# Reordered SBUF reservations in a macaron block: where TensorE's operands start

## The reference

```
x = x + 0.5 * ffn(layernorm(x))
x = x + attention(layernorm(x))
x = x + 0.5 * ffn(layernorm(x))

ffn(x):  h = silu(x @ W1 * s1) * (x @ W2 * s2)      # 256 -> 1024
         h = gelu(h @ H1 * t1)                      # 1024 -> 1024
         h = gelu(h @ H2 * t2)                      # 1024 -> 1024
         return h @ W3 * s3                         # 1024 -> 256
```

## The kernel before

| array | role in TensorE | before | after |
|---|---|---|---|
| `w_in`, `wring` | stationary, float32r | 128 | 128 |
| `fT_hi`, `fT_lo` | moving, float32r | 480 | 128 |
| `h_hi`, `h_lo` | moving in the hidden layers, stationary in the output layer | 480 | 128 |
| `w_out3` | moving in the output layer | 128 | 704 |
| `wproj`, `wo` | moving, float32 | 128 | 128 |
| `aT`, `zT`, `z`, `a_hat` | float32: stationary, transposed, or moving in the first pass | 800 | 128 |
| `f_hat` | transposed | 480 | 128 |
| `xf` | none (DMA, VectorE, ScalarE) | 480 | 128 |
| `slot0` to `slot3` | first pass's weights only; else DMA, VectorE, GpSimd | 800 | 128 |

## Time and profile before

### The profile page before, as it was taken

One profiled execution on the slowest core, in us unless ns is written; L12 is line 12 of the kernel. 1 busy time (PEld: TensorE's weight loads), 2 busy tenths in 40 slices (PEclk: granted clock), 3 DMA queues, 4 the chain that ended last, 5 costly groups with the idle time before them and its releaser, 6 DMA issues.

```text
span 1608.1 us, 19160 instructions
## 1 busy us (share of the span) xinstructions
PE 1528.4 (95%) x6978; PEld 1224.9 (76%) x6978; DVE 1086.0 (68%) x1475; ACT 677.6 (42%) x1062; POOL 553.3 (34%) x402
## 2 busy tenths in 40 slices
PE   7689999999999999999999999999999999998998
PEld 6567888777777778787777877768788877786887
DVE  6323758894777686777876877778675978793322
ACT  7434445344343435344534353434343444352442
POOL 2003051535171607162526070533614245434020
PEclk9899999999999999999999999999999999999999
DMA  7662848666766494857765757557474776754332
GB/s 308 252 241 101 281 140 302 224 207 226 232 234 218 155 312 142 279 171 262 261 229 183 251 182 261 185 192 254 157 265 158 269 247 223 269 198 157 118 100 71
DMA packets 189218, 342.41 MB, mean 213 GB/s; under 512 B 15552, under 2 KB 138560, under 8 KB 188736
## 3 DMA queue, kind: packets, MB, share of 16 engines
q1 hardware_dynamic: 189120, 341.13, 62.1%
HBM read 319.05 MB, written 30.41 MB: 217 GB/s over the span
## 4 chain that ended last, share of the span: by engine, by line
PE 66%; DVE 12%; POOL 8%; DMA 7%; ACT 4%; issue 3%; SPq 0%; DVEq 0%; POOLq 0%; ACTq 0%
PE f_bank L1101 22%; PE f_bank L1102 22%; PE a_banks L1179 6%; PE f_bank L1030 4%; PE f_bank L1031 4%; DMA weights_hi<-in_ffn_w 3%; POOL acc L693 3%; PE f_bank L1130 2%; PE f_bank L1131 2%; DVE slot L935 2%; DVE slot L979 2%; DVE S L941 2%; POOL acc L690 2%; PE a_banks L1199 1%; POOL h_lo L707 1%
## 5 line engine op out<-in xcount | busy, mean ns | idle before, releaser
L1101 PE MATMUL f_bank<-h_hi,wring 128*128 128x512 f32 x2048 | 824.4, 403 | 31.1 <-POOL h_lo L707 12.4
L1102 PE MATMUL f_bank<-h_lo,wring 128*128 128x512 f32 x2048 | 813.6, 397 | 0.0
L1101 PEld LDWEIGHTS f_bank<-h_hi,wring 128*128 128x128 f32 x2048 | 387.6, 189 | 131.9 <-issue 18.4
L1102 PEld LDWEIGHTS f_bank<-h_lo,wring 128*128 128x128 f32 x2048 | 387.6, 189 | 93.2 <-issue 1.4
L773 ACT ACTIVATE h_hi<-f_bank,colv 128x512 fp32r<-128x512 f32 x256 | 176.5, 689 | 553.1 <-PE f_bank L1102 552.9
L895 DVE TENSOR_TENSOR h_lo<-f_bank,h_hi 128x512 fp32r<-128x512 f32 x256 | 175.2, 687 | 258.5 <-ACT f_bank L774 256.8
L707 POOL TENSOR_TENSOR h_lo<-f_gated,h_hi 128x512 fp32r<-128x512 f32 x128 | 165.4, 1305 | 449.1 <-ACT h_hi L767 448.3
L1030 PE MATMUL f_bank<-fT_hi,w_in 128*128 128x512 f32 x480 | 197.5, 411 | 11.6 <-ACT f_gated L762 5.4
L1031 PE MATMUL f_bank<-fT_lo,w_in 128*128 128x512 f32 x480 | 191.5, 399 | 0.0
L979 DVE TENSOR_TENSOR slot<-slot,a_banks 128x1280 f32<-128x1280 f32 (+4 forms) x124 | 169.5, 1375 | 21.1 <-DMA slot<-keys_and_values 20.7
L935 DVE TENSOR_TENSOR slot<-slot,a_banks 128x1280 f32<-128x1280 f32 (+4 forms) x124 | 170.5, 1375 | 17.0 <-DMA slot<-keys_and_values 16.8
(11 more groups left out here) (117 smaller groups left out, 1328.1 us busy)
## 6 DMA issues: line engine op xcount, KB each, us to landing
wring<-weights_hi SPq DMA_DIRECT2D x256, 512.0 KB, 4.6
slot<-keys_and_values SPq DMA_DIRECT2D x128, 384.0 KB, 4.9
slot<-keys_and_values SPq DMA_DIRECT2D x64, 640.0 KB, 4.0
slot<-keys_and_values SPq DMA_DIRECT2D x312, 128.0 KB, 4.4
slot<-keys_and_values SPq DMA_DIRECT2D x64, 256.0 KB, 5.7
weights_hi<-in_ffn_w SPq DMA_DIRECT2D x16, 512.0 KB, 5.0
keys_and_values<-kv_out SPq DMA_DIRECT2D x32, 256.0 KB, 2.3
xf<-in_x SPq DMA_DIRECT2D x8, 512.0 KB, 5.8
```

Of the source, the lines that this page charges most:

```text
L1101: pe.matmul(bank[:, :], hi, h_hi[src][:, k, :], start=(k == 0), stop=False)
L1102: last = pe.matmul(bank[:, :], hi, h_lo[src][:, k, :], start=False, stop=(not general and k == KH - 1))
```

## The change

The order of the `sb(...)` calls is changed, and with it where each array starts; no array's size, and no instruction, is changed. The arrays whose sizes are whole KB are reserved first, and the small ones after them. `ident` (512 bytes), `half_neg` (16 bytes, taking 32) and `flag` (4 bytes, taking 32) come ahead of `w_out3`, which so starts 576 bytes further beyond a whole KB than the rest. The words that come with the change call the first arrays "at whole KB" and `w_out3` "64 bytes past one"; by adding up the sizes they are all 128 bytes past a whole KB, and `w_out3` is 704 past one.

```diff
--- before.py
+++ after.py
@@ -165,19 +165,11 @@
             return ctx.enter_context(nc.semaphore(name))
 
 
+
         w_in = sb("w_in", [P, IN_BLOCKS, WBLK], fp32r)
-        w_out3 = sb("w_out3", [P, OUT_BLOCKS, WBLK], fp32r)
         wring = sb("wring", [P, 4, WBLK], fp32r)
         wproj = sb("wproj", [P, KD, 4 * D])
         wo = sb("wo", [P, KD, D])
-        colv = sb("colv", [P, 4 * KH])
-        rowv = sb("rowv", [P, 6 * D + HEADS * (NU + NT)])
-        ident = sb("ident", [P, P])
-        differ = sb("differ", [P, BLOCKS])
-        differ_sum = sb("differ_sum", [P, 1])
-        ones = sb("ones", [P, 1])
-        flag = sb("flag", [1, 1], mybir.dt.int32)
-        half_neg = sb("half_neg", [P, NB])
 
         xf = sb("xf", [P, 2, NB, D])
         f_hat = sb("f_hat", [P, NB, D])
@@ -186,12 +178,6 @@
         h_hi = [sb(f"h_hi{i}", [P, KH, TT], fp32r) for i in range(2)]
         h_lo = [sb(f"h_lo{i}", [P, KH, TT], fp32r) for i in range(2)]
         f_gated = sb("f_gated", [P, 3, TT])
-        f_st = sb("f_st", [P, NB, 6])
-        f_mo = sb("f_mo", [P, 5, NB])
-        f_mean = sb("f_mean", [P, NB])
-        f_shift = sb("f_shift", [P, NB])
-        f_var = sb("f_var", [P, NB])
-        f_rs = sb("f_rs", [P, NB])
 
         xa = sb("xa", [P, 2, SB, D])
         aT = sb("aT", [P, KD, ST])
@@ -199,12 +185,19 @@
         kv_out = sb("kv_out", [P, SB, 2, D])
         slots = [sb(f"slot{g}", [P, GS, D]) for g in range(4)]
         a_hat = sb("a_hat", [P, SB, D])
-        S = sb("S", [P, SB, HEADS, NU])
         acc = sb("acc", [P, GS, D])
         z = sb("z", [P, SB, D])
         zT = sb("zT", [P, KD, ST])
 
         first_T = [aT, zT]
+        ident = sb("ident", [P, P])
+
+        half_neg = sb("half_neg", [P, NB])
+        flag = sb("flag", [1, 1], mybir.dt.int32)
+        w_out3 = sb("w_out3", [P, OUT_BLOCKS, WBLK], fp32r)
+        colv = sb("colv", [P, 4 * KH])
+        rowv = sb("rowv", [P, 6 * D + HEADS * (NU + NT)])
+        S = sb("S", [P, SB, HEADS, NU])
         merge = sb("merge", [P, 3, HEADS, NT])
         a_st = sb("a_st", [P, SB, 6])
         a_mo = sb("a_mo", [P, 5, SB])
@@ -214,6 +207,15 @@
         a_rs = sb("a_rs", [P, SB])
         mx = sb("mx", [P, SB, HEADS])
         sm = sb("sm", [P, SB, HEADS])
+        f_st = sb("f_st", [P, NB, 6])
+        f_mo = sb("f_mo", [P, 5, NB])
+        f_mean = sb("f_mean", [P, NB])
+        f_shift = sb("f_shift", [P, NB])
+        f_var = sb("f_var", [P, NB])
+        f_rs = sb("f_rs", [P, NB])
+        differ = sb("differ", [P, BLOCKS])
+        differ_sum = sb("differ_sum", [P, 1])
+        ones = sb("ones", [P, 1])
 
         fb = [ctx.enter_context(nc.psum_tensor(f"f_bank{i}", [P, 512], fp32)) for i in range(4)]
         pairs = [ctx.enter_context(nc.psum_tensor(f"a_banks{i}", [P, WBLK], fp32)) for i in range(2)]
```

## The result

The changed kernel takes 1588.38 us, the median of four runs (1587.78 to 1590.15); the kernel before took 1611.9 us in the runs beside it (1610.43 to 1613.33). The ratio is 0.9861, with a 95% interval of 0.9847 to 0.9875: 23.5 us or 1.4% less. The profiled execution took 1588.57 us.

What follows compares the result with a forecast made beforehand. PE's pace was taken to bound the kernel, a third of the span hanging on attention and transfers. 1609.98 - 28.4 gave 1581.6 us, 1582 us on the runs' scale, all else counted at nothing; range 1541 to 1613 us.

Steps and rivals of the forecast that it cites:

- What bounds the kernel: Whole kernel: PE, busy 95% of 1608.1 us, sets the end; a third of the span hangs on attention and transfers.
- Step 1: Hidden and input layers: moving operands going from 480 to 128 save 8.0 ns a matmul, bounds nothing to 17.3 ns.
- Theory A: Experiments' expectation: the moving operand's start within a 64-byte piece costs one more piece of 16 columns, 6.7 ns.
- Step 2: Chain: 3549 hidden and input matmuls at 8.0 ns shorten the path by 28.4 us; the other 1507 count nothing.
- Step 3: Output layer: w_out3 from 128 to 704, h from 480 to 128; counted at nothing, bound 6.4 us either way.
- Step 4: Everything else that moves (xf, xa, gate, kv_out, slots, acc): counted at nothing, a few us of gain as bound.
- Nothing happens: Rival, all float32r matmuls: columns are fed slightly slower than one per cycle wherever they start; 1611 us, chance 0.28.
- The whole excess goes: Rival, hidden, input and output layers: distance between moving and stationary starts matters, up to 17.3 ns a matmul; 1541 us, chance 0.17.
- Slower: Rival, hidden and input layers: streams starting at the same offset meet and wait, 8.0 ns a matmul; 1639 us, chance 0.13.

Runs made afterwards that it cites:

- both_crooked: The changed kernel with fT, h, w_in and wring, both operands of the hidden and input layers, at 160 instead of 128: 1588.06 us.
- weights_crooked: The changed kernel with the weights w_in and wring alone 32 bytes further, at 160 instead of 128: 1610.19 us.
- weights_64: The changed kernel with the weights w_in and wring alone 64 bytes further, at 192, fT and h at 128: 1610.56 us.
- moving_64: The changed kernel with the moving arrays fT and h alone 64 bytes further, at 192, weights at 128: 1599.83 us.
- moving_only: The kernel before with only xf, f_hat, fT, h and f_gated moved from 480 to 128; w_out3 and the attention's arrays stay: 1592.42 us.
- moving_crooked: The changed kernel with the moving arrays fT and h alone 32 bytes further, at 160 instead of 128: 1609.65 us.

## Why the prediction was right, and where not

**What bounds the kernel** held. PE's pace was what the change touched, no other engine's sum moved, and the difference in PE's busy time, 29.6 us, is more than the difference in the span, 21.4.

**Step 1, the price and its reason.** The size was near: forecast 8.0 ns a matmul, measured 6.7 in steady rows (233.3 to 226.7). Over the run it is less still: the hidden average went from 233.4 to 227.1 ns, 6.2, the input layer's from 233.4 to 228.6, 4.8, because a row of matmuls does not start at its new pace. In the trace of the kernel after, the first step behind float32 work or behind a break (a step of 260 ns or more) averages 232 to 235 ns, the fourth 228 to 230, and from about the tenth on it is 227. 4096 x 6.2 + 960 x 4.8 ns = 30.0 us, which is PE's 29.6. The reason was wrong. "I take them for the start" is the sentence that failed: the 8.0 ns between the output layer's excess and the hidden layer's are no price of a crooked moving operand. both_crooked has both operands crooked and runs at 226.7 ns; weights_crooked has a straight moving operand and runs at 233.3. What counts is the distance between the two starts. Theory A's 6.7 ns hit the number, but no run shows its reason, and two refute its condition: both_crooked has the moving operand 32 bytes past a multiple of 64 and runs at 226.7 ns, weights_64 has every start on a multiple of 64 and runs at 233.3. Why the difference is 6.7 ns, no run shows. The kernel after profits because its distance is 0; with its weights 32 bytes off (weights_crooked) the steps are 233.3 ns and the time is 1610.19 us.

**Step 2, what of it shortens the path.** It said that 3549 of 5056 matmuls, 0.70, would shorten the span. Measured: 21.4 of 29.6 us in the two profiles, 0.72; by the medians 23.5 of 30.0, 0.78. With the prices averaged over the run, 2998 x 6.2 + 551 x 4.8 ns = 21.2 us; the interval of the measured gain is 20.1 to 24.7 us. One pair of profiles is little to go by, but PE's idle time (span less busy) tells the same in all 14 kernels: 86.0 to 88.9 us, 87.0 on average, in the six with a hidden distance of 0, and 79.7 to 83.4 us, 81.3 on average, in the seven with hidden averages of 232.7 ns or more (moving_64 has 86.3). By that 5.7 of the 29.6 us are lost in waits, and the share is 0.8. So the step was right in kind and a little low. What was to be late next, the attention's chain and the ring's fills, is in the waits: GpSimd, `a_hat`, the ring's transfers. One of its signs did not come: the chain shares of VectorE and GpSimd were to rise, and they are 11% for 12% and 8% as before; it is the hidden layers' share that rose, from 43.5 to 44.3%. The 2998 hidden matmuls counted on the old chain are therefore not a fixed set.

**Step 3, the output layer at nothing:** 118.7 to 117.9 ns at the end, 118.2 to 117.8 on average, 0.2 us over the 596 matmuls of its chain share. But for its own reason: with `w_out3` left at 128 it would have gone to 119.9 (moving_only). The distance of 576, 64 within 256, saves those 2 ns, 1.2 us on the same 596 matmuls.

**Step 4, everything else at nothing:** held as far as it shows. With the hidden and input layers' distance at 32 and all other arrays at their new place the time is the old one (moving_crooked, 1609.65 us). The transfers into the slots, which start at 128 instead of 800 now, land their 384 KB in 4.7 us instead of 4.9, and not a good 1 us sooner; those into the ring take 4.7 instead of 4.6. One entry of the table of offsets is wrong, without effect on this: `z` and `zT` lie behind `S`, which has 2560 bytes, so before the change they start at 288 and not at 800.

**The rivals.** "Nothing happens" was wrong: the hidden layers' steps went from 233.3 to 226.7 ns, and the excess depends on where the operands start (20.0 ns at a distance of 96, 13.3 at 0). "The whole excess goes" had the right quantity, the distance of the two streams, but the wrong size: at least 13.3 of the hidden layer's 20.0 ns remain at every distance tried. It took the distance without its sign, though. The output layer's moving operand starts 352 bytes before the stationary one, which is 160 within 256; in the other stages it starts 352 behind it, which is 96. Its counter-argument, that loads at 128 and at 640 make no difference, was sound as a reading, and misled: they differ by 512, two whole periods of 256. "Slower" had the right place with the sign turned: 0 is the best distance for 512 columns (226.7 ns); but for the output layer it is, with 96, the worst of eight (119.9 ns), so such a case lay in the same kernel. Where the stationary operand starts does count: moving the weights alone by 32 bytes makes the matmuls' steps 6.7 ns longer (weights_crooked, 233.3 ns). That the two reads wait for each other was the author's reading, and is not shown: no run took one of them away.

The forecast of 1582 us was 6 us low. The price explains it: at the averaged prices the 3549 matmuls give 21.2 us and not 28.4. Some 2 us came back, as a little more of PE's gain reached the path than was counted.

## What to carry to other kernels

This was measured in one kernel and for two shapes. Where TensorE streams float32r at full clock (1.00 in these stretches), with a weight load for each matmul (6978 of each here), look at the distance between the start addresses of the moving and the stationary operand, within 256 bytes: for 512 columns 0 was the best of the eight multiples of 32 (226.7 ns against 233.3), for 256 columns 32 (116.7 against 119.9), and the difference is 3% of the pace in either. It costs only the order of the reservations: put arrays of whole KB together and the small ones behind them, and set one pad where a stage wants another distance. Read the pace from distances between starts in a stretch where no other engine is busy; and of a gain in PE's pace count only the part that lies on the chain, here 0.7 to 0.8.

## What the runs showed that was not expected

- The pace of float32r matmuls hangs on the distance of the two operands, with a period of 256 bytes: hidden steps of 226.7 ns at distances 0 and 256, 233.3 or close to it at 32, 96, 128, 192 and 224, 228.8 at 64. The absolute place does not matter (with all operands at 128, 160 and 0 beyond a whole KB the hidden averages are 227.1, 227.1 and 227.2 ns).
- The best distance is not the same for 512 and for 256 columns: at 0 the one has its shortest steps and the other its longest, 119.9 ns against 116.7 at 32.
- 13.3 ns over the estimated 213.3 remain at best, while float32 matmuls of 256 columns, at 216 ns, have only 2.9 over it. A float32 column takes about twice as long: 256 more take 213 ns (429 less 216), in float32r 107.4 (moving_only). No run told what these 13 ns are.
- A row of float32r matmuls reaches its 226.7 ns only at about its tenth step: behind float32 work or a break (a step of 260 ns or more) the first averages 232 to 235 ns, and behind the output layer the first seven average between 224 and 235. In the kernel before no such settling shows: its steps average between 229 and 237 ns at every place in a row. No run told why.
- Float32 matmuls take 216 ns for 256 columns and 429 for 512 at both distances that they had, 96 and 0.
